# Attention layer with two score sets: three buffers in place of two for the accumulated values

## What is computed

```python
def _L3_attn_ref(x, W_Q, W_K, W_V, W_K_prime, W_O, alpha):   # HEADS 16, HEAD_DIM 16, SCALE 4
    q = _heads(x @ W_Q.T, B, T)
    k = _heads(x @ W_K.T, B, T)
    v = _heads(x @ W_V.T, B, T)
    kp = _heads(x @ W_K_prime.T, B, T)
    scores = jnp.einsum('bhqd,bhkd->bhqk', q, k) / SCALE
    attn = jax.nn.softmax(scores, axis=-1)
    out_std = jnp.einsum('bhqk,bhkd->bhqd', attn, v)
    scores_p = jnp.einsum('bhqd,bhkd->bhqk', q, kp) / SCALE
    attn_p = jax.nn.softmax(scores_p, axis=-1)
    out_p = jnp.einsum('bhqk,bhkd->bhqd', attn_p, v)
    out = alpha * out_std + (1.0 - alpha) * out_p
    out = out.transpose(0, 2, 1, 3).reshape(B, T, C)
    return out @ W_O.T
```

## Time and profile before

| | |
|---|---|
| runs | 3952.14 us median of 3 (3947.62 to 3953.11) |
| profiled execution | 3942.6 us, span 3940.7 us |
| PE busy over the span | 3307.3 us (84%) |
| VectorE, ScalarE, GpSimd busy | 2546.4, 2033.6, 1890.6 us |
| the loop of this section, units 1 to 31 | about 3219 to 3706 us of the span |
| in it: PE, VectorE, ScalarE busy | 414.09, 245.43, 228.43 us of 487.00 |
| in it: granted PE clock | 0.88 of full speed |

### The profile page before, as it was taken

One profiled execution on the slowest core, in us unless ns is written; L12 is line 12 of the kernel. 1 busy time (PEld: TensorE's weight loads), 2 busy tenths in 40 slices (PEclk: granted clock), 3 DMA queues, 4 the chain that ended last, 5 costly groups with the idle time before them and its releaser, 6 DMA issues. The chain is left out here.

```text
span 3940.7 us, 61249 instructions
## 1 busy us (share of the span) xinstructions
PE 3307.3 (84%) x20068; PEld 2464.3 (63%) x20068; DVE 2546.4 (65%) x3859; ACT 2033.6 (52%) x4424; POOL 1890.6 (48%) x1639
## 2 busy tenths in 40 slices
PE   1869989989986888888888888988888888888867
PEld 0669866668974666666666666766655655545534
DVE  6431155553127999999999999999997345555431
ACT  0332223341227777787777777777774344444411
POOL 0123200000316988988898898888985000000044
PEclk9979999999998999999999999999999988988855
DMA  3069710003951111111111111111110000000045
GB/s 98 2 225 333 249 50 1 1 23 116 329 200 33 44 36 42 33 44 34 44 46 44 36 44 34 44 33 42 36 44 22 14 1 1 1 1 1 3 132 153
DMA packets 133783, 263.17 MB, mean 67 GB/s; under 512 B 13872, under 2 KB 104360, under 8 KB 122952
## 3 DMA queue, kind: packets, MB, share of 16 engines
q1 hardware_dynamic: 122120, 228.06, 17.5%
q0 software_dynamic: 11328, 30.95, 2.4%
HBM read 232.46 MB, written 26.51 MB: 66 GB/s over the span
## 5 line engine op out<-in xcount | busy, mean ns | idle before, releaser
L2109 POOL TENSOR_TENSOR ssm_hc<-ssm_hs,ssm_cb 128x1024 f32<-128x1024 f32 x512 | 1204.4, 2356 | 176.8 <-PE ssm_py L2223 155.3
L2609 DVE TENSOR_TENSOR_SCAN ssm_hs<-ssm_da,ssm_pb 128x512 f32<-128x512 f32 x1024 | 1221.5, 1207 | 96.4 <-POOL ssm_hc L2109 91.4
L2223 PE MATMUL ssm_py<-ssm_hc,ident 128*128 128x256 f32 x4096 | 1068.4, 384 | 37.9 <-POOL ssm_hc L2109 37.9
L2422 ACT ACTIVATE ssm_da<-ssm_dt,ssm_an 128x255 f32<-128x255 f32 x2048 | 863.7, 498 | 192.5 <-DVE ssm_hs L2609 154.5
L2223 PEld LDWEIGHTS ssm_py<-ssm_hc,ident 128*128 128x128 f32 x4096 | 709.3, 192 | 118.0 <-POOL ssm_hc L2109 46.1
L2590 DVE TENSOR_TENSOR ssm_pb<-ssm_pb,ssm_dtu 128x512 f32<-128x512 f32 x832 | 563.0, 677 | 44.0 <-PE ssm_pb L2210 23.1
L2210 PE MATMUL ssm_pb<-ssm_bst,ssm_eyeb 96*128 96x256 bf16 x1664 | 328.1, 279 | 140.7 <-DVE ssm_hs L2609 122.1
L2210 PEld LDWEIGHTS ssm_pb<-ssm_bst,ssm_eyeb 96*128 96x128 bf16 x1664 | 133.3, 99 | 346.6 <-DVE ssm_hs L2609 248.4
L1758 DVE TENSOR_REDUCE duo_mxr<-duo_pairs 128x4 f32<-128x1024 f32 x128 | 156.7, 1225 | 184.3 <-PE duo_pairs L1496 159.2
L3435 DVE TENSOR_TENSOR moe_hid<-moe_pu,moe_actg 128x512 f32<-128x512 f32 x71 | 49.1, 692 | 348.9 <-PE moe_pu L3078 348.9
L3078 PEld LDWEIGHTS moe_pu<-moe_xt,moe_up 128*128 128x128 f32 x2272 | 266.5, 193 | 6.4 <-ACT moe_xt L3198 3.0
(11 more groups left out here) (587 smaller groups left out, 5477.7 us busy)
## 6 DMA issues: line engine op xcount, KB each, us to landing
moe_up<-in_moe_up SPq DMA_DIRECT2D x72, 1024.0 KB, 5.0
ssm_cb<-ssm_c_dram SPq DMA_DIRECT2D x64, 1024.0 KB, 5.6
moe_down<-in_moe_down SPq DMA_DIRECT2D x72, 512.0 KB, 5.9
sw_wt<-in_sw_w SPq DMA_DIRECT2D x47, 192.5 KB
moe_x_dram<-moe_tok SPq DMA_DIRECT2D x32, 128.0 KB
moe_yg<-moe_y_dram SPq DMA_DIRECT2D x16, 256.0 KB, 3.0
tok_w<-in_wd SPq DMA_DIRECT2D x4, 576.0 KB
out<-h SPq DMA_DIRECT2D x1, 2056.0 KB, 7.1
```

The lines of the kernel that those rows point to most:

```text
L2109: nc.gpsimd.tensor_tensor(hc[:, n % 2, part_], hs[:, n % 2, part_], cb[:, q % 2, part_, :], ALU.mult).then_inc(s["hc_done"], 1)
L2223: ins = nc.tensor.matmul(sums(j), k.ident[:], hc[:, n % 2, st, :], start=False, stop=(q == QN - 1 and st == NQ_ - 1 and j % 2 == 1))
L2422: ins = nc.scalar.activation(da[:, n % 2, 2 * m + o, 1:L], dt2[:, v, j, 1:L], ACT.Exp, scale=a_n[:, d, j, st:st + 1])
L2609: nc.vector.tensor_tensor_scan(two(hs[:, n % 2, 2 * m:2 * m + 2, :]), two(da[:, n % 2, 2 * m:2 * m + 2, :]), two(pb[:, p % 4]), 0.0, ALU.m ...
```

## The change

`os_` gets a third buffer. All accesses go by `u % 3`, and `take_values` waits for L1800 of unit `u - 3` in place of `u - 2`. `rc`, which is filled from `os_`, keeps its two buffers and its waits. No instruction is added, taken out or moved.

```diff
@@ -1326,7 +1326,7 @@
-        os_, rc = sb("os", [P, 2, A, 256]), sb("rc", [P, 2, A, 256])
+        os_, rc = sb("os", [P, 3, A, 256]), sb("rc", [P, 2, A, 256])
@@ -1668,9 +1668,9 @@
                 def take_values(u, a):
                     ua = u * A + a
                     act.wait_ge(s["av_done"], ua + 1)
-                    if u >= 2:
-                        act.wait_ge(s["og_in"], u - 1)
-                    nc.scalar.copy(os_[:, u % 2, a, :], po[:, a, 0:256]).then_inc(s["os_in"], 1)
+                    if u >= 3:
+                        act.wait_ge(s["og_in"], u - 2)
+                    nc.scalar.copy(os_[:, u % 3, a, :], po[:, a, 0:256]).then_inc(s["os_in"], 1)
@@ -1780,19 +1780,19 @@
-                    nc.vector.stream_shuffle(rc[:, u % 2].rearrange("p a t -> p (a t)"), os_[:, u % 2].rearrange("p a t -> p (a t)"), [DH - DH * (u % 2)] * 32).then_inc(s["spread_in"], 1)
+                    nc.vector.stream_shuffle(rc[:, u % 2].rearrange("p a t -> p (a t)"), os_[:, u % 3].rearrange("p a t -> p (a t)"), [DH - DH * (u % 2)] * 32).then_inc(s["spread_in"], 1)
 
                 def scale_first(u):
...
-                    nc.vector.scalar_tensor_tensor(out=t1[:], in0=os_[:, u % 2, 0, :], scalar=alm[:, 0, u % 2:u % 2 + 1], in1=rc[:, u % 2, 0, :], op0=ALU.mult, op1=ALU.mult)
+                    nc.vector.scalar_tensor_tensor(out=t1[:], in0=os_[:, u % 3, 0, :], scalar=alm[:, 0, u % 2:u % 2 + 1], in1=rc[:, u % 2, 0, :], op0=ALU.mult, op1=ALU.mult)
 
                 def scale_second(u):
...
-                    o, rec = os_[:, u % 2], rc[:, u % 2]
+                    o, rec = os_[:, u % 3], rc[:, u % 2]
```

## The result

The changed kernel takes 3815.56 us (median of 4, 3808.94 to 3830.15) against 3949.88 us (median of 4) for the kernel before: ratio 0.967, 95% interval 0.9634 to 0.9707. Two repeats, on two chips, gave 0.966 (0.9593 to 0.9726) and 0.9698 (0.9664 to 0.9731).

The account below looks back on a forecast made before the run. The bound was taken to be PE's own work plus a once-a-unit detour through ScalarE's waiting copy. Gains of 69.7 + 33 - 5 = 98 us off 3942.6 gave 3844.6, plus 9.5 to the median: 3854 us, range 3830 to 3896.

Parts of the forecast that it names:

- term 2: PE's clock in the loop: without stalls it no longer falls to 1.2 GHz; 33 of 37.4 us gained, none for the tail.
- The detour through the copy: Once a unit, ScalarE's copy waits for L1800, delaying the exponential that frees PE's score bank; waiting for unit u - 3 removes it.
- Term 1: PE's stalls before score matmuls until the late exponential: 69.7 us in 30 stalls go, 9.0 of them in the tail.
- term 3: Score pairs that come late next, behind VectorE's norm or exponentials: 5 us taken back, bounded by 2 and 12.
- Rival (a): The stalls go but the clock's falls stay: gain 65 us, 3887 us; chance 0.14.
- (b): Another wait, for the score banks, takes the old one's place: gain 50 us, 3902 us; chance 0.11.
- (c): The change doesn't do what it says, as another signal to the copy comes as late: 3952 us; chance 0.03.
- (d): Slower: the dense loop is granted 1.2 GHz, up to 4156 us if held low throughout; chance 0.04.
- The median: The runs' median lies 9.5 us above the profiled execution's 3942.6; this was kept, taking 3844.6 to 3854 us.

Follow-up runs that it names:

- before_fill5: The kernel before with five useless matmuls put into each PE stall of units 3 to 30, the copy's wait kept: 3884.08 us against 3938.72, ratio 0.9857.
- after_fill2: The changed kernel with eight useless matmuls a unit put in ahead of PE's wait for the column bank: 3916.55 us against 3972.69 for the kernel before.
- before_again: The kernel before, run again unchanged for a second trace: 3961.89 us in one run, beside a median of 3944.0.

## Why the prediction was wrong

The direction, the place and the mechanism held. The step that failed is the size of term 2, what the slower clock costs: 33 us were put down, and 56 were measured.

- *The detour through the copy is the bound, and one wait further back removes it.* Right. The wait for L1800 is gone, the period is 48.92 us an image against the 48.9 worked out from four undisturbed stretches. The four places differ (11.8, 12.0, 12.4, 12.7), since the copy no longer hangs on VectorE, but their sum was the right thing to read.
- *Term 1, stalls, 69.7 us, less term 3, 5 us.* The sum is right: PE's idle time in the section fell from 81.5 to 17.1 us in the mean of three traces each, 64.4, where 64.7 was forecast. In the loop it fell by 62.1 - 2.6 = 59.4 at equal instructions, where the stalls were 60.7. That term 3 fits so well is luck, for the 5 us taken back are not where I put them, in score pairs of the loop that come late: no pair waits there (VectorE ends the norm of unit 6 at 3298.1, its next maximum begins 0.3 us after it could, and PE's following pair has that much slack). About 4 of the 5 lie in the tail, where the idle time fell by 5.0 us and not by the 9.0 of its four stalls. Exponentials still hold PE's score pairs up there, by 3.1 us:

```profile
3565.24 0.48 PE L1492 MATMUL duo_pairs<-duo_k,duo_q 32*128 32x256 f32 x2 [0.90 <-ACT duo_ex L1666]
...
3570.47 0.67 PE L1492 MATMUL duo_pairs<-duo_k,duo_q 32*128 32x256 f32 x2 [1.14 <-ACT duo_ex L1666]
...
3588.22 1.13 PE L1496 MATMUL duo_pairs<-duo_q,duo_k 32*128 32x256 f32 x8 [0.64 <-ACT duo_ex L1666]
```

- *Term 2, the clock, 33 us.* This is the step that failed. PE's busy time in the section, with the same instructions, fell from 468.1 to 411.8 in the mean: **56.3 us**. At equal instructions 41.0 of it are the loop's (40.6, 48.3 and 34.2 by trace), 14.8 the tail's and 0.5 those of the units ahead. Two choices of mine made it 33. I took 4 off the 37.4 of the loop for falls that might come without a stall; there were none, the clock was 1.00 in all three traces. And I took nothing for the tail, because PE lacks work there anyway; but its busy time fell from 53.4 to 38.6 in the mean. In the first trace of each kernel it was 49.16 and 39.76:

```profile
3650.74:3714.10 63.36, 49.16 (x344) 28.61 (x340) 22.58 (x56) 22.52 (x35) 0.00 (x0) 0.73 0.00 1
...
3562.25:3610.40 48.15, 39.76 (x344) 23.45 (x340) 22.55 (x56) 22.86 (x35) 0.00 (x0) 0.87 0.01 1
```

The tail's clock rose to 0.87 to 0.93 from 0.56 to 0.72: what PE does between its waits there is work too, and was done at the lower clock. The remaining 3.6 us are what the 37.4 were short of the loop's 41.0. The check on the rate was right: 0.47 to 0.48 us for each microsecond at 1.2 GHz in the three old loops (40.6 / 85, 48.3 / 102, 34.2 / 72), where the prediction had 0.45. A half, as the Trainium skill has it (TensorE: Matmul & The Clock Gate, Terms), is close to it, and by the skill's half I would have added 5 us.

- *Rival (a), the falls stay by short idles between groups*: did not come. The loop has none of PE's score-bank waits and no fall. What the Trainium skill says there of short idles between groups (TensorE: Matmul & The Clock Gate, A second HAM failure mode: psum-queue depth-cycling) was not seen here: the 13 waits of 0.4 us or less that before_fill5 has in its loop brought no fall either.
- *Rivals (b), (c), (d)*: (b) is ruled out by after_fill2, (c) by the waits, (d) by 317 us at 1.00 with PE busy 99% of it (313.85 of 316.47).
- *The median.* I kept the 9.5 us between profile and median. With the section's 120.7 in place of 98 the forecast would have been 3831, at the edge of the range; the remaining 15 us to 3815.56 I put down to scatter between executions and chips, which the range did not hold at its low end; no run traces them to one place. The clock's falls are chance from one execution to the next, 34 to 48 us in the loop alone, and a single trace of the kernel before could not tell that.

## What to carry to other kernels

A stall of a busy TensorE can be dearer than its length: here 64 us of stalls had 56 us of slower clock beside them, and both went with one more buffer of 2 KB a partition. Size the second part by PE's busy time at equal instructions between a disturbed and an undisturbed stretch, over the tail as well, and take several traces, for here it moved from trace to trace where the stalls did not (34 to 48 us against 62 of idle time in the loop, each time). When a copy waits for an old reader, look at what stands behind the copy in its queue: the 0.37 us copy harmed no one, the exponential two places later did.

## What the runs showed of the hardware

- Matmuls with no use, put into TensorE's stalls, kept its granted clock at 1.00 and made the kernel before 1.4% faster.
- Stalls of 2.1 to 2.5 us in a loop where PE was else busy brought a fall to 1.2 GHz in about half of the cases (14, 16 and 13 of 26 in three traces); with stalls half as frequent it was 5 of 13 in one trace, and the clock's cost per stall was 0.7 us in place of 1.6.
- The last expert layer runs at 1.2 GHz almost throughout, in both kernels, though PE is shown as busy for 88% to 98% of the time (before_again has it busy 116.96 us of 119.00 at 0.50; busy times of PE are modelled). Why isn't known:

```profile
3673.00:3790.00 117.00, 112.50 (x371) 67.32 (x372) 19.95 (x47) 32.82 (x91) 87.33 (x90) 0.54 0.60 171
...
3725.00:3862.00 137.00, 120.05 (x373) 69.72 (x374) 19.86 (x47) 33.00 (x92) 87.92 (x91) 0.52 0.53 146
```

- It is that layer, and not the change, that makes the difference behind the section. The stretch behind the section took 225 to 227 us in three traces of one chip (the second row) and 207 to 210 in six of two others (the first row is after, whose chip isn't known, as before's isn't). Each chip was used in one session only, so chip and hour can't be told apart. On the slow one the gathers' loop moves 146 GB/s against 171, and VectorE, at the copy of the turned rows, stands 57.0 us, 14 times, for something that the trace only calls remote; in after it stands there for PE alone. The trace of before shows the same as the slow chip's (49.0 us, 12 times). What differs is not settled. A comparison of two single traces would have put these 19 us down to the change.
